# The end of a fused convolution and feed-forward kernel: its last three steps written out, the last one in halves of four pairs

## What is computed

```python
x = x + conv_block(ln_c(x), w_pc, w_in, fft_w, w_out)
t = to_tokens(x)                                # one token per pixel, 48 channels
t = t + ffn(ln_t(t), W1, b1, W2, b2)
# conv_block: 3x3 convolution of the first 12 channels, 1x1 to 254 channels,
#   rfft2 of every 8x8 patch times fft_w, irfft2, gelu(a) * b, 1x1 back to 48
# ffn: two linear layers (48 -> 192 -> 48); inputs and weights rounded to a float
#   of 5 exponent and 2 mantissa bits, sums to 10 mantissa bits; relu between
```

## Time and profile before

| what | us |
|---|---|
| median of 3 runs | 719.0 (718.56 to 719.1) |
| the profiled execution, its own time | 720.83 |
| its span, first to last instruction | 718.9 |
| granted clock of TensorE, mean | 0.983 |

### The profile page before, as it was taken

How to read it: one execution, slowest core, us unless ns; L and a number is a source line. 1 busy time by engine, 2 the same in 40 slices (tenths; PEclk the granted TensorE clock), 3 DMA queues, 4 the chain that set the end, 5 groups by cost and what they waited for, 6 DMA issues and landing times.

```text
span 718.9 us, 19183 instructions
## 1 busy us (share of the span) xinstructions
PE 670.5 (93%) x6699; PEld 521.3 (73%) x6699; DVE 600.7 (84%) x1141; ACT 541.3 (75%) x1077; POOL 480.8 (67%) x354
## 2 busy tenths in 40 slices
PE   1579999999999999999999999999999999999973
PEld 1467788777777887778777877778777877777741
DVE  5436789888889898998999999888899899977785
ACT  3144578878888888888888888888888887777774
POOL 2752667877767777877777778777777778753351
PEclk9989999999999999999999999999999999999995
DMA  3342332333434432343334333434433324331111
GB/s 76 90 101 69 85 83 68 88 102 85 106 90 105 103 92 70 100 95 96 101 97 106 98 80 80 106 91 100 94 103 105 102 55 100 87 99 43 29 30 53
DMA packets 46486, 62.22 MB, mean 87 GB/s; under 512 B 19039, under 2 KB 34871, under 8 KB 46391
## 3 DMA queue, kind: packets, MB, share of 16 engines
q1 hardware_dynamic: 45143, 60.91, 33.7%
q10 hardware_dynamic: 1248, 0.08, 0.1%
HBM read 44.62 MB, written 16.35 MB: 85 GB/s over the span
## 4 chain that ended last, share of the span: by engine, by line
PE 76%; DVE 8%; POOL 7%; issue 3%; DMA 2%; ACTq 1%; ACT 1%; SPq 1%; DVEq 0%; POOLq 0%
PE inva L474 15%; PE mixp L461 14%; PE invb L481 14%; PE misc L673 7%; PE misc L490 5%; POOL st L1262 5%; PE misc L545 4%; PE misc L511 4%; PE misc L606 3%; PE misc L658 3%; PE misc L596 2%; PE misc L520 2%; DVE st L1176 2%; DVE qpix L1066 1%; PE misc L568 1%
## 5 line engine op out<-in xcount | busy, mean ns | idle before, releaser
L1009 DVE TENSOR_TENSOR gmix<-mixp,freq_w 128x508 f32<-128x508 f32 x256 | 162.9, 677 | 10.1 <-PE mixp L461 10.1
L474 PE MATMUL inva<-inv,gmix 128*127 128x128 f32 x1024 | 138.8, 279 | 0.2 <-DVE gmix L1009 0.2
L481 PE MATMUL invb<-inv,gmix 128*127 128x128 f32 x1024 | 135.5, 275 | 0.1
L474 PEld LDWEIGHTS inva<-inv,gmix 128*127 128x127 f32 x1024 | 127.0, 192 | 8.6 <-issue 7.8
L461 PE MATMUL mixp<-win,zh 60*128 60x254 f16 x1024 | 120.9, 273 | 5.2 <-DVE gmix L1009 3.5
L481 PEld LDWEIGHTS invb<-inv,gmix 128*127 128x127 f32 x1024 | 124.6, 192 | 0.7 <-DVE hbuf L1020 0.3
L461 PE MATMUL mixp<-win,zl 60*128 60x254 f16 x1024 | 119.6, 269 | 0.0
L1262 POOL TENSOR_TENSOR st<-st,neg_half 128x16 f32<-128x16 f32 x32 | 92.8, 2901 | 36.1 <-DVE st L1185 36.1
L759 ACT ACTIVATE hid<-misc 128x512 f16<-128x512 f32 x186 | 100.9, 599 | 18.2 <-PE misc L545 18.2
L1295 POOL TENSOR_TENSOR st<-st,neg_half 128x16 f32<-128x16 f32 x32 | 98.6, 3080 | 16.8 <-DVE st L1092 16.8
L745 ACT ACTIVATE gact<-inva 127x512 f32<-127x512 f32 x128 | 76.9, 601 | 36.2 <-PE inva L474 36.2
(11 more groups left out here) (122 smaller groups left out, 1223.2 us busy)
## 6 DMA issues: line engine op xcount, KB each, us to landing
xin<-in_x_dram SPq DMA_DIRECT2D x64, 192.0 KB, 3.4
xres<-in_x_dram SPq DMA_DIRECT2D x64, 192.0 KB, 4.2
out_dram<-ob SPq DMA_DIRECT2D x62, 192.0 KB, 2.7
taps<-cz_scratch SPq DMA_DIRECT2D x32, 292.5 KB
crm<-rm_scratch SPq DMA_DIRECT2D x64, 96.0 KB
cz_scratch<-cz SPq DMA_DIRECT2D x64, 48.8 KB
cx<-in_x_dram SPq DMA_DIRECT2D x32, 96.0 KB
rm_scratch<-rm_t SPq DMA_DIRECT2D x120, 4.0 KB
```

The source lines that it names most:

```text
L474: mm = pe.matmul(inva[0:HID, q * PX:(q + 1) * PX], gmix[:, s % 2, q, 0:HID], inv[:], start=True, stop=True, skip_group_check=True)
L481: mm = pe.matmul(invb[0:HID, q * PX:(q + 1) * PX], gmix[:, s % 2, q, HID:HID2], inv[:], start=True, stop=True, skip_group_check=True)
L1009: dve.tensor_tensor(gmix[:, s % 2, 2 * q:2 * q + 2, 0:HID2], mixp[q][:, 0:2 * HID2].rearrange("p (e c) -> p e c", e=2), freq_w[:], ALU.mul ...
```

## The change

Iterations 0 to 34 stay as they are. The general loop now ends before iteration 35 (`DRAIN` = 35), `late_step` and its special cases go, and each engine gets a `drain()` that writes out the rest: `OLDER` = 29, `OLD` = 30, `NEW` = 31.

- For step 31 projection, residual, transposes, norm, centring, power, scaling, both layers, bias, sum and store are in two halves of four pairs. Steps 29 and 30 have both layers, bias and sums in halves too; the store stays whole for them.
- Projection half 0 of step 31 is issued ahead of its last inverse. The second layer's half 0 of step 29 stands between the two parts of that inverse.
- The third bank of each first-layer half is copied and converted by VectorE, the other two by ScalarE; for step 31 VectorE also converts the second. Each half has other PSUM banks.
- POOL sums the halves of steps 29 and 30 (before: VectorE 29, POOL 30); VectorE sums step 31's halves from `zh`, into which ScalarE now copies the sums of step 31.
- SyncE stores steps 29 and 30 (the latter from `xres[:, 1]`); ScalarE issues four stores for step 31, two for each half, as 48 x 8 rows of 64 values.

The diff, cut to what the text speaks of:

```diff
@@ sync
             run(sp, step)
-            sp.wait_ge(out_stored, 32 * STEPS)
+            for l, done in ((OLDER, ob[:]), (OLD, xres[:, 1, :])):
+                sp.wait_ge(out_ready, OLDER + 2 * (l - OLDER) + 2)
+                for j in range(2):
+                    sp.dma_start(ov[image(l), l % SPI, j], done[HALF * j:HALF * j + CH, :]).then_inc(out_stored, 16)
+            sp.wait_ge(out_stored, 32 * (STEPS + 1))
@@ tensor
+            def drain():
...
+                t = (0, DRAIN)
+                pe.wait_ge(lo_ready, 2 * STEPS)
+                pe.wait_ge(h_ready, 4 * NEW + 2)
+                project_half(0, bank[3])
+
+                def between():
+                    pe.wait_ge(hid8_ready, 6 * OLDER + 3)
+                    second_layer_half(0, mixp[0])
+
+                inverse(t, 4, 3, between)
+                pe.wait_ge(hid16_ready, 6 * OLD)
+                turn_rest_half(0, bank[2])
+                pe.wait_ge(qpix_ready, OLD + 1)
+                turn_tokens_half(0, bank[0])
+                turn_tokens_half(1, bank[1])
                 pe.wait_ge(h_ready, 4 * STEPS)
+                project_half(1, mixp[1])
+                pe.wait_ge(hid8_ready, 6 * OLD)
+                pe.wait_ge(y16_ready, 2 * OLDER + 1)
+                second_layer_half(1, mixp[0])
...
+                first_layer(OLD, 0, (bank[0], bank[2], invb))
+                turn_rest_half(1, bank[3])
...
+                first_layer(OLD, 1, (bank[1], inva, mixp[1]))
...
+                turn_tokens_half(0, bank[0])
...
+                first_layer(NEW, 0, (bank[2], invb, bank[3]))
...
+                second_layer_half(0, mixp[0])
...
+                turn_tokens_half(1, bank[1])
+                pe.wait_ge(late_hid16, 2)
+                first_layer(NEW, 1, (bank[0], mixp[1], bank[1]))
...
+                second_layer_half(1, inva)
...
+                second_layer_half(0, bank[2])
...
+                second_layer_half(1, invb)
@@ scalar
+                for g in range(3):
+                    convert(OLDER, 0, g)
+                convert(OLDER, 1, 0)
+                gelu((0, DRAIN), 4, 3)
+                convert(OLDER, 1, 1)
+                convert(OLDER, 1, 2)
+                act.wait_ge(out_ready, OLDER)
+                sum_half(OLDER, 0, mixp[0], y16)
+                rest_half(0, bank[2])
+                tokens_half(OLD, 0, bank[0])
+                tokens_half(OLD, 1, bank[1])
+                sum_half(OLDER, 1, mixp[0], y16)
...
+                for half in range(2):
+                    act.wait_ge(late_out, half + 1)
+                    c0 = HALF * half
+                    for j in range(2):
+                        act.dma_start(ov[image(NEW), NEW % SPI, j].rearrange("c (r w) -> c r w", w=W)[:, :, c0:c0 + HALF],
+                                      xres[HALF * j:HALF * j + CH, 0, :].rearrange("c (r w) -> c r w", w=W)[:, :, c0:c0 + HALF])\
+                           .then_inc(out_stored, 16)
@@ vector
+                residual_half(0, bank[3])
+                scale_tokens(t)
+                gate(t, 4, 3)
+                bias_half(OLDER, 0, y16)
+                norm_half(0)
+                accumulate(OLD, 0, invb, hid8_ready, 6 * OLDER + 3)
+                bias_half(OLDER, 1, y16)
+                norm_half(1)
+                scale_half(0)
+                relu_part(OLD, 0, 0)
+                relu_part(OLD, 0, 1)
+                convert(OLD, 0, 2)
+                accumulate(OLD, 1, mixp[1], hid8_ready, 6 * OLDER + 6)
+                relu_part(OLD, 1, 0)
+                relu_part(OLD, 1, 1)
+                scale_half(1)
+                convert(OLD, 1, 2)
...
+                bias_half(OLD, 1, y16)
+                bias_half(NEW, 0, zh)
+                output_half(0)
+                bias_half(NEW, 1, zh)
+                output_half(1)
@@ gpsimd
+                centre_half(0)
+                power_half(0)
+                pool.wait_ge(out_stored, 32 * OLDER)
+                output_half(OLDER, 0, ob[:])
+                centre_half(1)
+                power_half(1)
+                output_half(OLDER, 1, ob[:])
+                pool.wait_ge(tch_ready, 2 * STEPS)
+                for c in range(2):
+                    output_half(OLD, c, xres[0:SPAN, 1, :])
```

377 lines of the change are left out of this document (225 added, 152 removed).

## The result

| | before | changed |
|---|---|---|
| median of 7 runs each (lowest to highest), us | 718.82 (718.07 to 719.54) | 713.86 (713.09 to 716.32) |
| ratio, 95% interval | | 0.9943 [0.9927, 0.9960] |
| span of the profiled execution, us | 718.9 | 714.4 |

The kernel is 4.96 us faster by these medians; 715.9 had been forecast. In a second comparison, against 17 runs of before, the same kernel had 713.88 and 717.57, ratio 0.9949 [0.9932, 0.9966], 3.7 us faster. The changed kernel's two medians differ by 0.02 us and before's by 1.25, so the difference between the two comparisons comes from before's runs. Part of it is in neither kernel's last steps, as the traces show.

A forecast was written before the change was run, and what follows sets the result against it. No engine is full from 694 us on: a drain, one step's chain of dependent work. A last sum 3.2 us earlier less 0.1 for the store takes 3.1 off the 718.9 span, 715.8, so median 715.9; range 713.2 to 718.4.

The forecast's parts named there:

- Part 1: Step 31's projection half 0 ahead of the last inverse: it ends at 688.6, the last gate 0.6 us later, at 691.5.
- Part 2: Step 31's norm in halves: POOL's first half power takes 1.65 us and ends at 696.1; the whole one ended at 700.4.
- Rival 1: POOL's power does not halve and takes 3.08 us for each half: median 718.7, no change; chance 0.13.
- Part 3: VectorE's scaling of half 0, queued behind half 1's norm, starts at 698.55, 2.4 us after its power; most lead unused.
- Part 4: Both layers of steps 30 and 31: VectorE is the path from 698.55 to its last cast at 708.4; before, 710.70.
- Rival 2: POOL and VectorE halves do not collide on the shared port: walk ends at 708.3, median 712.7; chance 0.08.
- The walk: Method laying each engine's new order over traced durations; instructions start when queue and producers allow, with holds at the shared port.
- Part 5: Last half: bias and sum end at 711.6, with 0.5 added for small gaps 712.1, which is 3.2 us earlier.
- Part 6: Step 31's store from ScalarE in 256-byte rows: tail 3.6 to 4.0 us, taken as 3.7, a loss of 0.1.
- rival 3: The last stores queue, so the tail grows by 1.4 us: 717.3; chance 0.11.
- Rival 4: 256-byte rows make the kernel slower, needing 62 ns for each packet; 722.1 at 80 ns; chance 0.06.
- the estimate from the page: Read-modify-write of rows under 512 bytes doubles the last half's transfer, adding some 0.9 us: 716.8.

The follow-up runs named there:

- again: The changed kernel run once more with nothing edited: median 713.88 us against 717.57 before, ratio 0.9949.
- sum_later_scale_early: Changed kernel with POOL's first half sum of step 29 behind half 1's power and VectorE's half 0 scaling ahead of half 1's norm: 715.93 us, ratio 0.9958.
- power_twice: Changed kernel with each half power issued twice on POOL: 716.07 us against 718.34 before, ratio 0.9969.
- store_whole: Changed kernel with SyncE storing step 31 in two pieces of 4 KB rows after both halves: 713.65 us against 717.57 before, ratio 0.9948.
- small_sums: Changed kernel with POOL's output half sums of steps 29 and 30 cut to 16 columns, most outputs left out: 712.03 us, ratio 0.9932.
- sum_later: Changed kernel with POOL's first half sum of step 29 moved behind the second centring and power: 714.41 us against 718.34 before, ratio 0.9946.
- store_split: Changed kernel with two of ScalarE's four half stores of step 31 issued by SyncE: 713.70 us against 718.34 before, ratio 0.9933.
- gated: Changed kernel with POOL's second half sum of step 29 waiting until VectorE has scaled half 1: 713.06 us against 717.61 before, ratio 0.9935.

## Why the prediction was right, and where it was off

**The size.** Forecast were 3.1 us off the span. Between the traces D gains 4.05 and T gives back 0.35, which leaves 3.7, and "again" measured 3.7 between medians. The other 1.3 of the first comparison's 4.96 are not explained by the last steps. They lie in before's median, which was 1.25 lower in the second comparison. D of before rests on one trace.

**Part 1** held. Undoing it alone cost 1.36 of D. The last gate came later than forecast: it ends at 691.41, which is 692.2 on the scale of the kernel before (0.8 are added to the changed kernel's times, the difference of the gates 2), against 691.5. No cost of that shows: half 0's mean starts at 691.74, when ScalarE's copy for it has just ended (691.71). Half 1's reduction ends 0.3 later than forecast (696.8 on that scale, against 696.5), and the wait for POOL's sum behind it takes that up.

**Part 2, the power's price** (1.65 from the columns, bounds 1.5 and 3.08) measured 1.64. It started at 694.60 on that scale, forecast 694.45. The second one took 2.03, 0.4 more than the forecast had. What stretches it stays open. It is not the scaling beside it, since in sum_later_scale_early none runs beside it and it takes 2.08. A relu pair beside it is not enough either, since step 30's power took its usual 3.08 with one wholly beside it (686.80 to 687.54). Rival 1, the power that does not halve, is excluded by the row, and power_twice gives its price, 2.5 us.

**Part 3** held: 2.2 us of lead unused, forecast 2.4, with the two holds at the places named. What it left open, whether the lead is worth having, sum_later_scale_early answers with no for the one order that was tried.

**Part 4** held to 0.2 us, in part by luck. The last cast ended at 708.2 on that scale, forecast 708.4. From the scaling to there the forecast had 7.65 us of work, two holds (1.51) and 0.66 of small waits. The trace shows 9.77 in all: one hold of 0.79, on the relu pair at 699.81, a wait of 0.44 for ScalarE's copy ahead of the relu at 705.72, which the sum did not have, and 0.89 of small waits. The second hold did not come, as POOL's sum at 704.73 fell beside a copy out of PSUM (0.69 at 704.58), which kept its length. That the clock adds nothing held for this order, as store_whole's trace shows above.

**The shared port.** Rival 2 (no collisions, 712.7) is excluded by the 0.67, 0.75 and 1.52 rows and by small_sums. The walk had 3.3 us for all holds (711.6 to 708.3) and 2.4 for those by POOL's sums; small_sums puts the latter at 1.4. The walk without holds had missed the path through ScalarE. The walk's rule, that no VectorE instruction on SBUF alone starts while POOL centres or sums, was wider than the rows. The half reduction took its 0.56 at 695.43, wholly beside POOL's sum at 695.40, and the earlier trace rows already had the full one (0.95 at 695.36) beside the centring. The Trainium skill (SBUF — State Buffer, SBUF: two separate sides) describes the ports that VectorE and GpSimd share as an exclusive lock, kept for the whole instruction by whichever starts first, where VectorE runs in a two-port mode or reads two operands from SBUF. The rows agree for POOL's sums and centrings: the reduction, with its one operand, is not held, and a relu of 0.35 us takes 1.24 and ends 0.16 us behind a sum of POOL's (700.97 and 700.81, in sum_later). They do not agree for the power: VectorE's sum of two operands ran beside it in its usual 1.23.

**Part 5 is where it was off**, in the main. The last sum came 0.85 us earlier than forecast. "0.5 short of the traced ... since it leaves out small gaps; I add them": the new order's walk needed no such addition. Its own end, 711.6, was 0.3 from the traced 711.26, while the corrected 712.1 was 0.8 off. So the term that was mis-sized is this 0.5. A likely reason, not tested, is that gaps on the old path, where engines wait for each other, do not carry over to a path that is mostly one busy engine. That the walk's own end came so near is also owed to the terms of Part 4 that made up for each other. Of the other 0.35, 0.2 was there at the last cast. In the rest POOL's sum did hold VectorE, but at 707.73, about a microsecond earlier than forecast on the common scale, so that it stretched VectorE's sum of half 0, while the second layer of the last half was still under way, rather than the last bias.

**Part 6** took 3.7 for the tail; measured 3.94, inside its 3.6 to 4.0. "Half 0's two are out of the way before half 1 is ready" held only just: half 0's issues began at 709.50, 0.96 us before the last sum ended, and ended with it. What the sum had too small is the issue itself: the third took 1.08, above the 0.37 to 0.76 that were allowed, and the fourth began at 711.6, 1.15 after the last sum. In store_whole the two issues take 0.95 us from 0.03 after the sum. By store_split not the issues but the landings, 0.5 us apart, set the tail. They do queue, as rival 3 had it, but not at its price: T is 0.35 above before's, not 1.4. Rival 4 did not come: a packet cost some 21 ns (14 to 29) by the queue lines, not the 62 that would have turned the sign, and store_whole, with few large packets, is at most 0.14 us shorter. The 0.9 us behind the estimate from the page stand on no row.

## What to carry to other kernels

At the end of a pipeline, halve the instruction whose time goes by its columns and on which everything waits, but count what each half is queued behind: here the first half's lead of 2.2 us was lost in order, and taking it back by order cost the second half more. When an instruction of POOL is moved off one collision, count what it will meet at its new place: sum_later moved the hold and saved nothing, and gated took 0.8 us off the second scaling, of which TensorE's queue let 0.17 through. And when run-to-run spread comes from a part of the program that an edit does not touch, compare lengths between fixed points of the traces, and look at the granted clock both ahead of the first point and between the two. The lengths repeated to 0.01 us over four traces with that same stretch, where medians of the same kernel differed by more than their intervals.
